# Attention times V in two layouts of its output tiles: rows interleaved by parity, or columns 0 to 127 of all 16 rows

## The chip, the core and the metric

The kernel runs on one core of one Trainium2 chip. The metric is device time in microseconds (us) of one execution; the median of several runs counts. The engines are TensorE (PE in the profile; its weight loads stand apart as PEld), VectorE (DVE), ScalarE (ACT), GpSimd (POOL) and SyncE (SP). SP and ACT also issue the transfers between the chip's main memory and the on-chip memory; all transfers run on the same 16 DMA engines.

## What is computed

The input `x` has 128 rows, 192 columns and 192 channels. After a group normalisation over all of `x`, a row attention gives each (row, column, head) a weight `sw`, and a column attention over the 192 columns, whose logits are summed over all rows, mixes the columns. The part that the change touches is the last line before the residual:

```
Q = (x @ Wq).reshape(B, R, C, H, D) * scaling * sw
K = (x @ Wk).reshape(B, R, C, H, D)
V = (x @ Wv).reshape(B, R, C, H, D)
QK = jnp.einsum('brihd,brjhd->bhij', Q, K)
attn = jax.nn.softmax(QK, axis=-1)                    # 12 heads of 192 x 192
out = jnp.einsum('bhij,brjhd->brihd', attn, V)        # 128 rows x 192 columns x 192 channels
x = x + out
```

## The kernel before, in words

**Halves.** The 12 heads of 16 channels are done in two halves `h` of 6 heads (`EH` = 96 channels). The first part of the kernel reads x, makes the statistics, and projects (L1195 and L1203) Q and K of half 0 and V of both halves, with V written to main memory. Then for each half: the logits (L1325 to L1329), softmax and transposed attention matrices `AT`, then attention times V (`attended`, L1290 and L1294). Between the two halves stands the second projection `project1` (again L1195 and L1203), which reads the transposed x back from main memory (`load_xt`, L414) in 24 chunks of 768 KB, four buffers `XT`, four chunks to a turn.

**Attention times V.** The output of a half is cut into 8 chunks `n` of `RI` = 16 rows. A chunk is 16 x 192 = 3072 (row, column) pairs of 96 channels; it lies in the tile `XO[n]` of 128 partitions x 3 thirds x 8 x 96. Before the change the flat pairs are cut into pieces of 128: third 0 has columns 0 to 127 of the even rows, third 2 columns 64 to 191 of the odd rows (held in place 1 of the tile's second index by the order `(0, 2, 1)`), and the middle third has columns 128 to 191 of an even row on partitions 0 to 63 and columns 0 to 63 of the next row on partitions 64 to 127. Each third moves between main memory and `XO[n]` in one transfer of 1024 runs of 384 bytes (384 KB).

A block is one chunk and one pair of heads; there are 24 blocks in a half (`BLOCK`; chunks 0 and 1 are interleaved, the others follow each other in threes). For each block PE makes two groups in two banks of its accumulation memory. The outer group (L1290, `t == 0`) has 2 heads x 2 thirds x 5 terms = 20 matmuls with a 128 x 128 stationary block of `AT` and 128 moving columns of V (8 rows x 16 channels). The middle group (L1294) has 2 heads x 5 terms x 2 partition halves = 20 matmuls with a 128 x 64 stationary block; the two of a pair work on different columns of the array. The five terms are high and low parts of fp16 pairs. DVE then adds each group to `XO[n]`: two instructions for the outer thirds (L1055), one for the middle (L1059).

**Order and queues.** All order is by hand, with semaphores. `load_x` (SP, L398) brings the residual x of a chunk into `XO[n]`: in half 0 chunks 0 and 1 among the last stores of V, 6 and 7 after them, then chunks 2 to 5 in turn with the loads of V (`load_v`, L428 and L430); in half 1 chunks 6 and 7 between the `load_xt` of the second projection, then 0 and 1, then 2 to 5 again with V. `store_out` (L357) writes a chunk when DVE has added its last block: the outer thirds wait for DVE's outer add, the middle third for its middle add. ACT's queue stores chunks 0 to 4, SP's queue 5 to 7. At the end of half 0 SP has first the four `load_xt` of turn 0 (which wait for the stores of chunks 0 and 1), then the stores of chunks 5 to 7, and behind these the `load_xt` of turn 1; a queue issues in program order.

Of the kernel before, what the change touches and what calls it, by code (L numbers as in the profile page):

```python
# [11 lines left out]
R, C, E, H = 128, 192, 192, 12  # L12
D = E // H
G, GC = 32, E // 32
P = 128
E1 = E - P
HALF = H // 2
EH = HALF * D
# [10 lines left out]
RI = 16  # L29
# [9 lines left out]
def row_column_attention(nc, x, wq, wk, wv, wqs, wks, res_mask, seq_mask, out):  # L39

    xs = x.rearrange("b r c e -> (b r) c e")
    xf = x.rearrange("b r c e -> (b r c) e")
    of = out.rearrange("b r c e -> (b r c) e")

    def by_thirds(flat, n, h):
        thirds = flat[n * RI * C:(n + 1) * RI * C, h * EH:(h + 1) * EH].rearrange("(q t p) e -> p t q e", t=3, p=P)
        return [thirds[:, t, :, :] for t in (0, 2, 1)]

    xt_dram = nc.dram_tensor("xt_scratch", [NCH, P, 3 * NQ * 2 * R], fp16, kind="Internal").ap()
    v0_dram = nc.dram_tensor("v0_scratch", [2, P, R, 2 * EH], fp16, kind="Internal").ap()  # L50
# [3 lines left out]
    with ctx:  # L54
# [25 lines left out]
        V0 = [q.rearrange("p w (r s e) -> p w r s e", s=2, e=EH) for q in V0]  # L80
# [67 lines left out]
        sp = [0]  # L148
# [190 lines left out]
        def attended_bank(m):  # L339

            return (m + 6) % 8
# [5 lines left out]
        opens = [min(j for j in range(NB) if BLOCK[j][0] == n) for n in range(NRC)]  # L347
        closes = [max(j for j in range(NB) if BLOCK[j][0] == n) for n in range(NRC)]

        I_FIRST, I_LAST = slice(0, P), slice(E1, C)  # L350

        def store_out(eng, h, n):
            eng.wait_ge(s_ad[h], 2 * closes[n] + 1)
            for t, third in enumerate(by_thirds(of, n, h)):
                if t == 2:
                    eng.wait_ge(s_ad[h], 2 * closes[n] + 2)
                eng.dma_start(third, XO[n][:, t, :, :]).then_inc(s_out[n], 16)  # L357

        block = ctx.enter_context(nc.Block())

# [1 line left out]
        def _(sp):  # L362
# [31 lines left out]
                                         VS[c % 2][:, :, h, k, :]).then_inc(s_vs[c % 2], 16)  # L394

            def load_x(h, n):
                for t, third in enumerate(by_thirds(xf, n, h)):
                    sp.dma_start(XO[n][:, t, :, :], third).then_inc(s_xl[n], 16)  # L398

            for c in range(3):  # L400
                store_xt(c)
# [31 lines left out]
            for h in range(2):  # L433
                if h:
                    for first, last, n in ((1, 2, 6), (2, 4, 7), (4, TURNS, 0)):
                        with sp.Fori(first, last) as t:
                            for b in range(4):
                                sp.wait_ge(s_pj[1], (4 * t + b - 3) * 2)
                                load_xt(4 * t + b, b)
                        if n:  # L440
                            sp.wait_ge(s_out[n], 48)
                            load_x(1, n)
                    sp.wait_ge(s_pj[1], NG1)
                    load_x(1, 0)
                    load_x(1, 1)
                for n in range(HALF):
                    sp.wait_ge(s_qk[h], n + 1)
                    load_v(h, n)
                    if n < len(IN_BIG):
                        load_x(h, n + 2)  # L450
                for n in range(HALF, NRC):
                    load_v(h, n)
                if h == 0:
                    for b in range(4):
                        sp.wait_ge(s_sp[b], 16 * (NCH // 4))
                    for n in range(2):
                        sp.wait_ge(s_out[n], 48)
                    for b in range(4):
                        load_xt(b, b)
                for n in range(HALF - 1, NRC):  # L460
                    store_out(sp, h, n)
            for k in range(NRC):
                sp.wait_ge(s_out[k], 96)

        @block.gpsimd
        def _(pool):
# [70 lines left out]
        def _(act):  # L537
# [167 lines left out]
            for h in range(2):  # L705
# [15 lines left out]
                if h:  # L721
                    body(0)
                    with act.Fori(1, TURNS // 2) as t:
                        body(t)
                    for n in IN_BIG:
                        act.wait_ge(s_out[n], 48)
                    with act.Fori(TURNS // 2, TURNS) as t:
                        body(t)
                    q_high1(NG1 - 1, 7)
# [23 lines left out]
        def _(dve):  # L753
# [230 lines left out]
            for h in range(2):  # L984
# [61 lines left out]

                for j, (n, hp) in enumerate(BLOCK):
                    if opens[n] == j:
                        dve.wait_ge(s_xl[n], 48 * (h + 1))
# [12 lines left out]

        @block.tensor
        def _(pe):
# [204 lines left out]
            def attended(h, m):  # L1269
                (n, hp), t = BLOCK[m // 2], m % 2  # L1270
                if t == 0:
                    pe.wait_ge(s_atl[h], 2 * hp + 2)
                    if opens[n] == m // 2:
                        pe.wait_ge(s_vl[n], 48 * (h + 1))
                when(pe, s_ad[h], m - 7)
                po = PS[:, attended_bank(m), :].rearrange("p (t q a d) -> p t q a d", t=2, a=2, d=D)

                def terms(k, odd, columns):
                    high, low = AT[:, k, :, columns], AT[:, k, :, C:2 * C][:, :, columns]
                    v0h, v0l = (V0[n][:, :, odd:RI // 2:2, s, k * D:(k + 1) * D] for s in range(2))  # L1280
                    v1 = V1[n][:, odd:RI:2, k * D:(k + 1) * D]
                    return ((high[:, 0, :], v0h), (high[:, 0, :], v0l), (low[:, 0, :], v0h),
                            (high[:, 1, :], v1), (low[:, 1, :], v1))

                for a in range(2):
                    k = 2 * hp + a
                    if t == 0:
                        for odd in range(2):
                            for i, (stationary, moving) in enumerate(terms(k, odd, I_LAST if odd else I_FIRST)):
                                ins = mm(po[:, odd, :, a, :], stationary, moving, start=i == 0, stop=i == 4)  # L1290
                    else:
                        for i, pair in enumerate(zip(terms(k, 0, slice(P, C)), terms(k, 1, slice(0, E1)))):
                            for odd, (stationary, moving) in enumerate(pair):
                                ins = mm(po[odd * E1:(odd + 1) * E1, 0, :, a, :], stationary, moving,  # L1294
                                         start=i == 0, stop=i == 4)
                ins.then_inc(s_av[h], 1)

# [71 lines left out]
```

## Time and profile before

| | us |
|---|---|
| three runs | 542.17, 542.51, 544.75; median 542.51 |
| the profiled execution, whole | 541.36 |
| its span (first to last instruction) | 539.6 |

The main stretches of the profiled execution, by the line numbers that run in them:

| stretch (us from the start of the span) | what PE does |
|---|---|
| 0 to 79 | transposes of x, statistics |
| 79 to 264 | first projection, scores |
| 267 to 312 | logits of half 0 |
| 312.6 to 360.4 | attention times V, half 0 |
| 360.3 to 437 | second projection, 6 turns of 4 chunks |
| 440.5 to 486 | logits of half 1 |
| 486.4 to 533.2 | attention times V, half 1 |
| 533.2 to 539.6 | last adds and stores |

In the views of the trace, a row of the timeline has a start, a length, the engine and line, the operation with its shape and count, and in brackets the idle time of the engine before it with what ended it. Equal neighbours are merged into one row. Rows of the chain of waits show, in order of time, what the end of the program waited for. In the tables by stretch, the last three columns are the granted clock of TensorE as a share of 2.4 GHz, the mean busy share of the 16 DMA engines (over 1 where their packets overlap), and the GB/s that they moved.

### The profile page before, as it was taken

The numbers are of one execution on the slowest core, as the hardware profiler recorded it, in microseconds if no ns is written. First come the engines' busy times: TensorE is split into PE (matmuls) and PEld (weight loads), VectorE is DVE, ScalarE is ACT, GpSimd is POOL, SyncE is SP. The second block draws the span as 40 slices with busy tenths as digits, with TensorE's granted clock in tenths as the row PEclk, the third lists the DMA queues.
The fourth block names the chain that finished last, engine by engine and source line by source line (L and its number), as shares of the span: only waits on it lengthen the run. The fifth ranks groups of instructions, "written<-read, shape, count | busy, mean of one in ns | idle before, by whom it ended". The sixth has DMA issues, their size and how long they took to land.

```text
span 539.6 us, 15989 instructions
## 1 busy us (share of the span) xinstructions
PE 502.7 (93%) x6319; PEld 393.6 (73%) x6319; DVE 390.7 (72%) x1046; ACT 276.7 (51%) x577; POOL 185.2 (34%) x232
## 2 busy tenths in 40 slices
PE   7797698899999999999899999999999979999995
PEld 6686554555555555555599988888899979998884
DVE  2689968898888888889736678655667644667763
ACT  4576776798999999995311210004565631211000
POOL 3000345585778787774300000004556540000000
PEclk9899989999999999999999999999999989999998
DMA  8999012744776667898999999999989657997997
GB/s 325 379 419 384 3 58 118 235 133 168 230 229 216 218 220 235 222 226 165 234 209 320 335 336 320 342 289 314 319 282 331 214 151 223 309 284 264 259 251 197
DMA packets 186271, 134.44 MB, mean 249 GB/s; under 512 B 168992, under 2 KB 170848, under 8 KB 186208
## 3 DMA queue, kind: packets, MB, share of 16 engines
q1 hardware_dynamic: 153664, 120.88, 71.8%
q10 hardware_dynamic: 32544, 12.68, 9.5%
q8 instruction: 44, 0.72, 0.6%
q14 instruction: 19, 0.16, 0.1%
HBM read 76.92 MB, written 56.62 MB: 247 GB/s over the span
## 4 chain that ended last, share of the span: by engine, by line
PE 76%; DVE 10%; DMA 5%; ACT 3%; issue 2%; SPq 1%; POOL 1%; DVEq 0%; POOLq 0%; ACTq 0%
PE PS L1195 23%; PE PS L1203 12%; PE PS L1290 11%; PE PS L1294 6%; DVE EXTRA L766 5%; DMA EXTRA<-in_x 4%; PE PS L1325 3%; PE PS L1328 3%; PE PS L1329 3%; PE PS L1326 3%; PE PS L1327 3%; DMA EXTRA<-xt_scratch 1%; PE PS L1156 1%; SPq L357 1%; PE PS L1079 1%
## 5 line engine op out<-in xcount | busy, mean ns | idle before, releaser
L1195 PE MATMUL PS<-WP,EXTRA 128*128 128x384 f16 (+1 forms) x1152 | 158.0, 286 | 2.6 <-DMA EXTRA<-xt_scratch 1.2
L1195 PEld LDWEIGHTS PS<-WP,EXTRA 128*128 128x128 f16 x1152 | 97.0, 98 | 46.1 <-issue 17.4
L492 POOL TENSOR_TENSOR EXTRA<-BIG,EXTRA 128x512 f16<-128x512 f32 x69 | 82.5, 1197 | 31.8 <-ACT EXTRA L597 23.9
L532 POOL TENSOR_TENSOR BIG<-EXTRA,BIG 128x384 f32 x48 | 43.8, 914 | 130.0 <-ACT BIG L708 126.6
L1203 PE MATMUL PS<-WP,EXTRA 64*128 64x384 f16 (+1 forms) x1152 | 83.1, 284 | 0.1
L1203 PEld LDWEIGHTS PS<-WP,EXTRA 64*128 64x128 f16 x1152 | 47.4, 94 | 29.4 <-issue 17.4
L498 POOL TENSOR_TENSOR BIG<-EXTRA,BIG 128x192 f16<-128x192 f32 x96 | 54.7, 570 | 36.6 <-ACT BIG L651 36.5
L1290 PE MATMUL PS<-BIG,EXTRA 128*128 128x128 f16 x960 | 61.9, 220 | 0.3
L715 ACT CAST BIG<-PS 128x384 f32 (+1 forms) x48 | 23.0, 479 | 73.3 <-PE PS L1203 64.3
L1290 PEld LDWEIGHTS PS<-BIG,EXTRA 128*128 128x128 f16 x960 | 53.8, 98 | 4.6 <-issue 0.5
L766 DVE BATCH_NORM_STATS2 EXTRA<-BIG 128x6 f32<-128x512 f32 x72 | 43.8, 678 | 16.1 <-ACT BIG L546 16.0
L1325 PE MATMUL PS<-BIG 128*128 128x192 f16 x192 | 48.8, 254 | 5.4 <-POOL BIG L532 3.2
L644 ACT CAST EXTRA<-PS 128x384 f16<-128x384 f32 x96 | 45.4, 473 | 13.9 <-PE PS L1203 6.1
L919 DVE TENSOR_TENSOR EXTRA<-PS,EXTRA 128x384 f16<-128x384 f32 x96 | 52.4, 546 | 0.0
L586 ACT ACTIVATE BIG<-BIG,small 128x512 f32<-128x512 f32 x63 | 50.9, 811 | 0.0
L993 DVE TENSOR_TENSOR EXTRA<-PS,SW 128x192 f32<-128x192 f32 x96 | 29.7, 349 | 28.2 <-ACT BIG L715 25.7
L1329 PE MATMUL PS<-BIG 128*128 128x192 f16 x192 | 48.3, 251 | 0.0
L1328 PE MATMUL PS<-BIG 128*128 128x192 f16 x192 | 48.2, 251 | 0.0
L1326 PE MATMUL PS<-BIG 128*128 128x192 f16 x192 | 48.2, 251 | 0.0
L1327 PE MATMUL PS<-BIG 128*128 128x192 f16 x192 | 48.2, 251 | 0.0
L902 DVE CAST BIG<-PS 128x192 f16<-128x192 f32 x96 | 34.0, 354 | 19.3 <-ACT EXTRA L644 18.9
L1096 PE MATMUL PS<-ident,EXTRA 128*128 128x128 f32 x288 | 37.8, 287 | 7.6 <-DMA EXTRA<-in_x 4.3
(178 smaller groups left out, 931.1 us busy)
## 6 DMA issues: line engine op xcount, KB each, us to landing
EXTRA<-in_x SPq DMA_DIRECT2D x24, 768.0 KB, 9.7
xt_scratch<-EXTRA SPq DMA_DIRECT2D x24, 768.0 KB, 3.3
BIG<-v_scratch SPq DMA_DIRECT2D x48, 384.0 KB, 5.3
EXTRA<-xt_scratch SPq DMA_DIRECT2D x24, 768.0 KB, 6.5
v_scratch<-EXTRA SPq DMA_DIRECT2D x32, 384.0 KB, 3.8
EXTRA<-in_x SPq DMA_DIRECT2D x24, 384.0 KB, 4.9
BIG<-in_x SPq DMA_DIRECT2D x24, 384.0 KB, 6.8
out_x<-BIG ACTq DMA_DIRECT2D x18, 384.0 KB, 5.6
```

Of the source, the lines that this page charges most:

```text
L492: pool.tensor_tensor(tt[:, t, 1, :].rearrange("p (q n) -> p q n", n=P), raw(c, t), tt[:, t, 0, :].rearrange("p (q n) -> p q n", n=P), ALU. ...
L498: pool.tensor_tensor(QA[:, :, C + 2 * s:C + 2 * s + 2, :], tq0(s).rearrange("p i k d -> p k i d"), QA[:, :, 2 * s:2 * s + 2, :], ALU.subtr ...
L766: ins = v.bn_stats(ST[:, t, c, :], raw(c, t))
L919: v.tensor_tensor(vs[:, :, :, 1, :], ps[:, :, 2 * EH:2 * EH + E].rearrange("p i (h e) -> p i h e", h=2), vs[:, :, :, 0, :], ALU.subtract)
L1195: ins = mm(outs[a], xt[:, t, s, q * P:(q + 1) * P], WP[:, t, w, wc], start=first and j == 0, stop=last and j == 2, skip_group_check=True)
L1203: ins = mm(outs[a], xt[rows, 1, s, q * P:(q + 1) * P], WP[rows, 1, w, wc], start=first and j == 0, stop=last and j == 2, skip_group_check= ...
L1290: ins = mm(po[:, odd, :, a, :], stationary, moving, start=i == 0, stop=i == 4)
L1325: mm(p0, q0, kh, start=first, stop=False, skip_group_check=True)
L1326: mm(p0, q0, kl, start=False, stop=last, skip_group_check=True)
L1327: mm(p1, q1, kh, start=first, stop=False, skip_group_check=True)
L1328: mm(p1, q1, kl, start=False, stop=last, skip_group_check=True)
L1329: ins = mm(p2, q2, kh, start=False, stop=last, skip_group_check=True)
```

## The change

`by_columns` takes the place of `by_thirds`. A chunk's 16 rows are two windows `w` of 8 rows. Places 0 and 1 of the tile now hold columns 0 to 127 of window 0 and window 1; the middle place holds columns 128 to 191, window 0 on partitions 0 to 63 and window 1 on partitions 64 to 127. A chunk moves in four transfers instead of three: two of 128 partitions (384 KB each) and two of 64 partitions (192 KB each). The counts that semaphore waits compare with go from 48 to 64 and from 96 to 128. All 16 rows have the same 128 output columns in the outer places, so the outer group has one stationary block for both, and its matmuls get 256 moving columns instead of 128: 10 matmuls instead of 20.

```diff
-    def by_thirds(flat, n, h):
-        thirds = flat[n * RI * C:(n + 1) * RI * C, h * EH:(h + 1) * EH].rearrange("(q t p) e -> p t q e", t=3, p=P)
-        return [thirds[:, t, :, :] for t in (0, 2, 1)]
+    def by_columns(full, tile, n, h):
+        rows = full[0, n * RI:(n + 1) * RI, :, h * EH:(h + 1) * EH].rearrange("(w r) p e -> w p r e", w=2)
+        return ([(rows[w, 0:P, :, :], tile[:, w, :, :]) for w in range(2)]
+                + [(rows[w, P:C, :, :], tile[w * E1:(w + 1) * E1, 2, :, :]) for w in range(2)])
...
-            for t, third in enumerate(by_thirds(of, n, h)):
+            for t, (there, here) in enumerate(by_columns(out, XO[n], n, h)):
                 if t == 2:
                     eng.wait_ge(s_ad[h], 2 * closes[n] + 2)
-                eng.dma_start(third, XO[n][:, t, :, :]).then_inc(s_out[n], 16)
+                eng.dma_start(there, here).then_inc(s_out[n], 16)
...
-                for t, third in enumerate(by_thirds(xf, n, h)):
-                    sp.dma_start(XO[n][:, t, :, :], third).then_inc(s_xl[n], 16)
+                for there, here in by_columns(x, XO[n], n, h):
+                    sp.dma_start(here, there).then_inc(s_xl[n], 16)
...
                     if t == 0:
-                        for odd in range(2):
-                            for i, (stationary, moving) in enumerate(terms(k, odd, I_LAST if odd else I_FIRST)):
-                                ins = mm(po[:, odd, :, a, :], stationary, moving, start=i == 0, stop=i == 4)
+                        for i, (stationary, moving) in enumerate(terms(k, slice(0, 2), slice(0, P))):
+                            ins = mm(po[:, :, a, :], stationary, moving, start=i == 0, stop=i == 4)
                     else:
-                        for i, pair in enumerate(zip(terms(k, 0, slice(P, C)), terms(k, 1, slice(0, E1)))):
-                            for odd, (stationary, moving) in enumerate(pair):
-                                ins = mm(po[odd * E1:(odd + 1) * E1, 0, :, a, :], stationary, moving,
+                        for i, pair in enumerate(zip(*(terms(k, w, slice(P, C)) for w in range(2)))):
+                            for w, (stationary, moving) in enumerate(pair):
+                                ins = mm(po[w * E1:(w + 1) * E1, 0:RI // 2, a, :], stationary, moving,
                                          start=i == 0, stop=i == 4)
```

On PE, attention times V of half 0 opens so before the change (PS is the accumulation memory, BIG holds V, EXTRA holds `AT`; L1309 to L1312 are transposes of the last attention matrix):

```order
L1290 MATMUL PS<-BIG,EXTRA 128x8x16 x20
L1294 MATMUL PS<-BIG,EXTRA 64x8x16 x20
L1290 MATMUL PS<-BIG,EXTRA 128x8x16 x20
L1294 MATMUL PS<-BIG,EXTRA 64x8x16 x20
L1290 MATMUL PS<-BIG,EXTRA 128x8x16 x20
L1294 MATMUL PS<-BIG,EXTRA 64x8x16 x20
L1309 MATMUL PS<-ident,EXTRA 128x128
```

and so with it, where the file's line numbers are 4 lower:

```order
L1286 MATMUL PS<-BIG,EXTRA 128x16x16 x10
L1290 MATMUL PS<-BIG,EXTRA 64x8x16 x20
L1286 MATMUL PS<-BIG,EXTRA 128x16x16 x10
L1290 MATMUL PS<-BIG,EXTRA 64x8x16 x20
L1286 MATMUL PS<-BIG,EXTRA 128x16x16 x10
L1290 MATMUL PS<-BIG,EXTRA 64x8x16 x20
L1305 MATMUL PS<-ident,EXTRA 128x128
```

Each outer group has half the matmuls, each twice as wide; the middle groups and their order are as before.

On SP, the stretch of half 0 that has the loads of x (EXTRA and BIG hold `XO`) and of V runs so before the change:

```order
L398 DMA EXTRA<-in_x 128x8x96 [waits xnT_stored3,projected0,v_stored1,v_stored0]
L398 DMA EXTRA<-in_x 128x8x96 x5
L428 DMA BIG<-v_scratch 128x1536 [waits logits_psum0]
L428 DMA BIG<-v_scratch 128x1536
L430 DMA BIG<-v_scratch 128x1536
L398 DMA BIG<-in_x 128x8x96 x3
```

and so with it:

```order
L395 DMA EXTRA<-in_x 128x8x96 [waits xnT_stored3,projected0,v_stored1,v_stored0]
L395 DMA EXTRA<-in_x 128x8x96
L395 DMA EXTRA<-in_x 64x8x96 x2
L395 DMA EXTRA<-in_x 128x8x96 x2
L395 DMA EXTRA<-in_x 64x8x96 x2
L425 DMA BIG<-v_scratch 128x1536 [waits logits_psum0]
L425 DMA BIG<-v_scratch 128x1536
L427 DMA BIG<-v_scratch 128x1536
L395 DMA BIG<-in_x 128x8x96 x2
L395 DMA BIG<-in_x 64x8x96 x2
```

Where three transfers of 128 partitions stood for a chunk, two of 128 and two of 64 stand; nothing moves past anything else. The stores on ACT's and SP's queues change in the same way.

## Rows read from the trace of the kernel before

**Rows 1.** The page: the span, and the chain that ended last by line.
```profile
span 539.6 us, 15989 instructions
...
PE PS L1195 23%; PE PS L1203 12%; PE PS L1290 11%; PE PS L1294 6%; DVE EXTRA L766 5%; DMA EXTRA<-in_x 4%; PE PS L1325 3%; PE PS L1328 3%; PE PS L1329 3%; PE PS L1326 3%; PE PS L1327 3%; DMA EXTRA<-xt_scratch 1%; PE PS L1156 1%; SPq L357 1%; PE PS L1079 1%
```
**Rows 2.** Chain in order of time, 355 to 392: start, us, what.
```profile
361.18 2.63 SPq L357
...
365.75 1.38 SPq L357
...
367.24 6.50 DMA EXTRA<-xt_scratch
```
**Rows 3.** Timeline of PE, 370 to 392: the two waits.
```profile
374.06 2.15 PE L1195 MATMUL PS<-WP,EXTRA 128*128 128x192 f16 x24 [1.24 <-DMA EXTRA<-xt_scratch]
...
387.89 2.15 PE L1195 MATMUL PS<-WP,EXTRA 128*128 128x192 f16 x24 [1.10 <-DVE BIG L999]
```
**Rows 4.** Timeline of SP's queue, 276 to 340: issues of x and of V.
```profile
276.92 5.69 SPq L398 DMA_DIRECT2D EXTRA<-in_x  x6
...
290.56 1.55 SPq L428 DMA_DIRECT2D BIG<-v_scratch  x2
```
**Rows 5.** Busy time by stretch, half 0; last columns clock, DMA share, GB/s.
```profile
284.00:312.00 28.00, 28.00 (x318) 26.67 (x316) 18.52 (x41) 6.04 (x15) 0.00 (x0) 1.00 1.06 329
312.00:326.00 14.00, 13.88 (x264) 12.02 (x265) 11.13 (x27) 2.04 (x5) 0.00 (x0) 1.00 1.00 347
326.00:340.00 14.00, 14.00 (x301) 12.53 (x300) 10.37 (x26) 0.00 (x0) 0.00 (x0) 1.00 1.14 298
...
361.00:369.00 8.00, 8.00 (x125) 7.53 (x124) 4.15 (x12) 3.25 (x7) 2.74 (x3) 1.00 1.24 286
```
**Rows 6.** Timeline, attention times V of half 1: PE and DVE.
```profile
527.41 1.29 PE L1290 MATMUL PS<-BIG,EXTRA 128*128 128x128 f16 x20
...
528.81 0.87 DVE L1055 SCALAR_TENSOR_TENSOR EXTRA<-PS,small,EXTRA 128x256 f32<-128x256 f32 x2 [0.70 <-PE PS L1290]
...
529.32 1.29 PE L1290 MATMUL PS<-BIG,EXTRA 128*128 128x128 f16 x20
```
**Rows 7.** Lines L1290 and L1195: ns min/median/max; one run of L1195, timeline.
```profile
L1290 PE MATMUL PS<-BIG,EXTRA x960: 216/219/231, 312.6 to 532.3; 128*128 128x128 f16 x192
...
L1195 PE MATMUL PS<-WP,EXTRA x576: 246/246/257, 360.3 to 437.0; 128*128 128x192 f16 x192
...
378.49 4.13 PE L1195 MATMUL PS<-WP,EXTRA 128*128 128x192 f16 x48
```
**Rows 8.** Busy time by stretch, end of half 1.
```profile
527.00:528.00 1.00, 1.00 (x29) 0.91 (x24) 1.00 (x3) 0.00 (x0) 0.00 (x0) 1.00 0.16 33
...
534.00:538.50 4.50, 0.00 (x0) 0.00 (x0) 0.00 (x0) 0.00 (x0) 0.00 (x0) 0.81 0.99 264
```
**Rows 9.** Busy time by stretch: stores of two queues; x loads alone.
```profile
353.00:355.00 2.00, 2.00 (x47) 1.80 (x48) 1.27 (x3) 0.00 (x0) 0.00 (x0) 1.00 1.26 288
...
279.00:285.00 6.00, 6.00 (x69) 5.60 (x68) 3.91 (x10) 1.32 (x3) 0.00 (x0) 1.00 1.17 325
```
**Rows 10.** Loads of weights: two stretches; ACT queue's bytes to 16.73; an issue.
```profile
16.25:16.73 0.48, 0.04 (x1) 0.00 (x0) 0.48 (x2) 0.40 (x1) 0.00 (x0) 1.00 1.11 340
16.73:17.50 0.77, 0.61 (x6) 0.61 (x7) 0.64 (x2) 0.77 (x1) 0.00 (x0) 1.00 1.14 281
...
q10 hardware_dynamic: 1034, 0.69, 12.9%
...
SW<-in_L_conv_Wv ACTq DMA_DIRECT2D x2, 48.0 KB, 8.3
```
**Rows 11.** Two idle times of PE (timeline), and the clock around the second.
```profile
266.68 0.30 PE L1325 MATMUL PS<-BIG 128*128 128x192 f16 x1 [2.24 <-POOL BIG L498]
...
440.48 0.30 PE L1325 MATMUL PS<-BIG 128*128 128x192 f16 x1 [3.19 <-POOL BIG L532]
...
440.00:446.00 6.00, 5.52 (x47) 5.53 (x48) 0.54 (x2) 0.00 (x0) 0.42 (x1) 0.72 1.17 324
```

More of the change, by code:

```diff
@@ L41, in row_column_attention @@
     xs = x.rearrange("b r c e -> (b r) c e")
-    xf = x.rearrange("b r c e -> (b r c) e")
-    of = out.rearrange("b r c e -> (b r c) e")
-    def by_thirds(flat, n, h):
-        thirds = flat[n * RI * C:(n + 1) * RI * C, h * EH:(h + 1) * EH].rearrange("(q t p) e -> p t q e", t=3, p=P)
-        return [thirds[:, t, :, :] for t in (0, 2, 1)]
+    def by_columns(full, tile, n, h):
+        rows = full[0, n * RI:(n + 1) * RI, :, h * EH:(h + 1) * EH].rearrange("(w r) p e -> w p r e", w=2)
+        return ([(rows[w, 0:P, :, :], tile[:, w, :, :]) for w in range(2)]
+                + [(rows[w, P:C, :, :], tile[w * E1:(w + 1) * E1, 2, :, :]) for w in range(2)])
     xt_dram = nc.dram_tensor("xt_scratch", [NCH, P, 3 * NQ * 2 * R], fp16, kind="Internal").ap()
@@ L348, in row_column_attention @@
         closes = [max(j for j in range(NB) if BLOCK[j][0] == n) for n in range(NRC)]
-        I_FIRST, I_LAST = slice(0, P), slice(E1, C)
         def store_out(eng, h, n):
             eng.wait_ge(s_ad[h], 2 * closes[n] + 1)
-            for t, third in enumerate(by_thirds(of, n, h)):
+            for t, (there, here) in enumerate(by_columns(out, XO[n], n, h)):
                 if t == 2:
                     eng.wait_ge(s_ad[h], 2 * closes[n] + 2)
-                eng.dma_start(third, XO[n][:, t, :, :]).then_inc(s_out[n], 16)
+                eng.dma_start(there, here).then_inc(s_out[n], 16)
         block = ctx.enter_context(nc.Block())
@@ L440, in _ @@
                         if n:
-                            sp.wait_ge(s_out[n], 48)
+                            sp.wait_ge(s_out[n], 64)
                             load_x(1, n)
@@ L456, in _ @@
                     for n in range(2):
-                        sp.wait_ge(s_out[n], 48)
+                        sp.wait_ge(s_out[n], 64)
                     for b in range(4):
@@ L462, in _ @@
             for k in range(NRC):
-                sp.wait_ge(s_out[k], 96)
+                sp.wait_ge(s_out[k], 128)
         @block.gpsimd
@@ L725, in _ @@
                     for n in IN_BIG:
-                        act.wait_ge(s_out[n], 48)
+                        act.wait_ge(s_out[n], 64)
                     with act.Fori(TURNS // 2, TURNS) as t:
@@ L1048, in _ @@
                     if opens[n] == j:
-                        dve.wait_ge(s_xl[n], 48 * (h + 1))
+                        dve.wait_ge(s_xl[n], 64 * (h + 1))
                     o = XO[n][:, :, :, hp * 2 * D:(hp + 1) * 2 * D]
@@ L1275, in attended, with terms @@
                 when(pe, s_ad[h], m - 7)
-                po = PS[:, attended_bank(m), :].rearrange("p (t q a d) -> p t q a d", t=2, a=2, d=D)
-                def terms(k, odd, columns):
+                po = PS[:, attended_bank(m), :].rearrange("p (q a d) -> p q a d", a=2, d=D)
+                def terms(k, ws, columns):
                     high, low = AT[:, k, :, columns], AT[:, k, :, C:2 * C][:, :, columns]
-                    v0h, v0l = (V0[n][:, :, odd:RI // 2:2, s, k * D:(k + 1) * D] for s in range(2))
-                    v1 = V1[n][:, odd:RI:2, k * D:(k + 1) * D]
+                    v0h, v0l = (V0[n][:, ws, :, s, k * D:(k + 1) * D] for s in range(2))
+                    v1 = V1[n].rearrange("p (w r) e -> p w r e", w=2)[:, ws, :, k * D:(k + 1) * D]
                     return ((high[:, 0, :], v0h), (high[:, 0, :], v0l), (low[:, 0, :], v0h),
```

## The prediction, on record before the result

> **What bounds the kernel now.** I read the page first, then the chain of waits in order of time, and then, for the places that the change touches, the timeline and the busy time by stretch. By the page PE carries the chain: the projections (L1195) and attention times V (L1290, L1294) are its longest pieces, and transfers hold only a few per cent [rows 1]. The few per cent are what matters here. In attention times V PE runs without a gap in both halves: an outer group begins every 1.91 us (529.32 less 527.41), and DVE idles 0.70 us before each pair of its outer adds [rows 6], so DVE has room and PE sets the pace.
>
> What follows each half differs. Half 1 ends with the program, and its DMA engines have room: busy share 0.16 in the microsecond at 527, before the stores of chunk 6, and only the stores of the last chunk run after PE has ended [rows 8]. Time saved on PE in half 1 is time saved. Half 0 ends in the second projection, whose turn 1 waits for its first `load_xt`: PE idles 1.24 us before 374.06, released by that transfer [rows 3]. The load was issued at 367.24, directly behind the last stores on SP's queue (issued at 361.18 to 365.75) [rows 2], whose issues last 1.4 to 2.6 us each: about what a transfer takes, so the queue takes a new one only as an old one drains. The DMA engines are at a share of 1.00 or more from 284 to 369 [rows 5], and SP's queue in this time goes from one issue to the next: the six x loads at 276.92 take 5.69 us to issue, and V's two loads at 290.56 take 1.55 [rows 4]. So from about 277 to 374 the time at which turn 1 starts is set by the sum of the DMA work, not by PE. Half 0's time saved on PE goes into that wait, and every microsecond added to the DMA work there comes out on the critical path.
>
> **The change part by part.**
>
> *Outer matmuls, fewer and wider.* A run of 20 takes 1.29 us with 0.219 us for its last: spacing (1.29 - 0.219)/19 = 56.4 ns for 128 columns. A run of 48 with 192 columns: (4.13 - 0.246)/47 = 82.6 ns [rows 7]. That is 26.2 ns for 64 columns, so 256 columns take 56.4 + 52.4 = 108.8 ns (an estimate: no such matmul is in this trace at the full clock). A block goes from 20 x 56.4 = 1.128 to 10 x 108.8 = 1.088 us, 0.04 us less. Halving the number buys little, since the columns that stream through are the same. In half 1: 24 x 0.04 = **-1.0 us**. In half 0 the same 1.0 us only lengthens the wait for turn 1: **0**.
>
> *Middle matmuls, DVE adds, waits.* Same counts and shapes; **0**. The fourth transfer of a chunk adds an issue on SP or ACT; behind the queue's backlog this is hidden, and the bytes and the number of 384-byte runs don't change.
>
> *The middle transfers, cut in halves of 64 partitions.* This is the disputed price. A whole x transfer of 393,216 bytes takes 1.21 us at the 325 GB/s of x loads alone, and a whole store 1.37 us at 288 GB/s [rows 9]. A half transfer costs between half of that (0.60 and 0.68 us: no loss) and all of it (a loss of 0.60 and 0.68 us, if half the partitions move at half the rate). The nearest row is in the loads of the weights, which have both kinds. ACT's queue loads Wq, Wk and Wv in pieces of 96, 48, 48 and 96 KB, the 48 KB ones on 64 partitions; 0.69 MB are through at 16.73, which is the first nine pieces, so that from there to about 17.5 it moves Wv's two 64-partition pieces beside SP's other loads. The rate falls from 340 to 281 GB/s [rows 10]. If half of the bytes there are 64-partition traffic, that traffic runs at 1/(2/281 - 1/340) = 239 GB/s, 1.42 times as long. The row does not isolate the cause (768-byte runs, SP's own pieces beside them), but nothing there speaks for a gain. I take 0.42: a loss of 0.25 us for each half of an x load, 0.29 us for each half of a store that has the engines to itself.
>
> The Trainium skill, SBUF — State Buffer, section "Door 1: The DMA port swizzle", speaks against the change: partitions 0 to 63 reach only half of the ports, 196 GB/s against 328 for 128 partitions at 1 MiB, and a transfer on each half one after the other gains nothing. By that ratio, 1.67, the sum below would end near 550.5 us.
>
> *Where that lands.* In half 0 all eight chunks' x is loaded ahead of turn 1's first load, by SP's queue alone: 16 halves x 0.25 = +4.0 us. Of the 16 halves of stores most run while the other queue moves whole transfers; with two queues at work the stores go at 288 GB/s, the whole engines' pace, so I count a quarter, those of chunk 2 and of chunk 7: 4 x 0.29 = +1.2. Turn 1 starts **+5.2 us** later. PE, idle 1.24 us before, idles some 7.4 (5.2 more, and 1.0 that half 0 saved). After idle times of 2.24 and 3.19 us the granted clock fell to half (1.2 GHz): the mean of the six microseconds from 440 is 0.72, so 0.28 x 6 = **+1.7 us** are lost [rows 11]; after 1.24 us it did not fall. The wait of 1.10 us at 387.89, before turn 2 [rows 3], should go, as loads have caught up by then while PE is later: **-1.1** (bounds 0 and -1.1). In half 1 x is loaded with room to spare, and the stores have room until the last chunk, whose two halves of the middle lie at the end: **+0.6**.
>
> **Sum** against the profiled execution's own 541.36 us: +5.2 + 1.7 - 1.1 + 0.6 - 1.0 = +5.4, so 546.8. That execution lies 1.15 us under the median of the three runs, 542.51; +5.4 on the median gives 547.9. **I forecast 548.0.**
>
> **The rivals.**
>
> *The halves cost no more than their bytes.* For it: the same runs, the same 16 engines, no fewer bytes in flight; the two halves follow each other on one queue and may overlap at the seam. Against it: the fall from 340 to 281. Then half 0 gains nothing up to turn 1, since the DMA work is the same; half 1 gains 1.0; the wait before turn 2 may shrink, or the wait before turn 1, then near 2.2 us, may cost clock: 541.0 to 543, likeliest 541.5, no change that can be measured. A loss under 0.15 us a half belongs here too, up to 545.
>
> *A half takes as long as a whole.* The upper bound of the same price: 16 x 0.60 + 4 x 0.68 = 12.3 for turn 1, then 12.3 + 1.7 - 1.1 + 1.4 - 1.0 = +13.3: 556.
>
> *Faster.* The other sign needs PE: if a 256-column matmul with one weight load cost only the slope, 2 x 52.4 = 104.8 ns, and the switch to the middle group (1.91 us less 1.128 and the middle's own 10 x 56.4 = 0.56, so 0.22 a block for two switches) halved as well, half 1 would gain 24 x (0.08 + 0.11) = 4.6 us: 538. It decides in half 1 alone, where PE sets the pace: an outer group under 0.98 us. Against it: the spacing already is that of streaming columns.
>
> **How the numbers follow.** About 0.5%, 2.7 us, is what a measurement of this kernel can tell from no change. Halves slower by 0.15 to 0.45 us each: 0.50, between 545 and 553, likeliest 548. No loss or a small one: 0.38, between 541 and 545. Halves as long as wholes: 0.08, 553 to 556. Faster: 0.04. The range leaves out most of the last two: 541.0 to 553.0. Faster by over 0.5%: 0.04; within 0.5%: 0.38; slower: 0.58.
>
> **What would show it.** Right: outer groups of 10 matmuls in a timeline row of about 1.25 us (9 x 108.8 ns and some 0.27 for the last); a GB/s under 300 where SP loads x alone (279 to 285 had 325); PE's wait before turn 1 at 5 to 9 us, put down to `xt_scratch`, with a clock of 0.5 for a few microseconds behind it; an unchanged pace of blocks in half 1 within 0.05 us. Wrong: x loads at 325 GB/s as before and a wait before turn 1 near 2.2 us, which means that the halves cost nothing; or a wait before turn 1 that moved while the rate stayed, which would put the loss in the issues of SP's queue instead; or a gain in half 1 of over 2 us, which would put my spacing wrong.

## The result, and the profile after

The changed kernel takes 547.38 us (median of 7 runs, 544.34 to 550.73); the kernel before, run beside it, 543.49 (7 runs, 538.31 to 548.07). The ratio is **1.0074**, with a 95% interval of 1.0037 to 1.0110: slower, by about 4 us, against a forecast of 548.0. The profiled execution of the changed kernel took 547.22 us with a span of 545.3; that of before, 541.36 with 539.6 [rows 1].

In the changed kernel all line numbers are three or four lower: stores are L354, loads of x L395, loads of XT L411, projections L1192 and L1200, the outer matmuls L1286, the middle ones L1290. The page of after, the chain by line:

```profile
span 545.3 us, 15061 instructions
...
PE PS L1192 22%; PE PS L1200 11%; PE PS L1286 10%; PE PS L1290 6%; DVE EXTRA L763 5%; DMA EXTRA<-in_x 4%; PE PS L1321 3%; PE PS L1325 3%; PE PS L1324 3%; PE PS L1323 3%; PE PS L1322 3%; DMA EXTRA<-xt_scratch 2%; ACTq L354 1%; PE PS L1153 1%; SPq L395 1%
```

Against [rows 1], `xt_scratch` has gone from 1% to 2%, and ACT's stores have come onto the chain. Where that is, the timeline of PE in the second projection of after shows (start, us, what, and in brackets the idle time before it with its releaser):

```profile
368.01 2.14 PE L1192 MATMUL PS<-WP,EXTRA 128*128 128x192 f16 x24 [2.45 <-DVE BIG L996]
...
378.87 4.02 PE L1192 MATMUL PS<-WP,EXTRA 128*128 128x192 f16 x24 [4.55 <-DMA EXTRA<-xt_scratch]
382.82 2.34 PE L1200 MATMUL PS<-WP,EXTRA 64*128 64x192 f16 x48
385.09 4.13 PE L1192 MATMUL PS<-WP,EXTRA 128*128 128x192 f16 x48
```
```profile
418.87 2.15 PE L1192 MATMUL PS<-WP,EXTRA 128*128 128x192 f16 x24 [0.86 <-DMA EXTRA<-xt_scratch]
```

The wait before turn 1, 1.24 us in [rows 3], is now 4.55, and the 24 matmuls behind it take 4.02 us where 24 take 2.15 elsewhere: they run at half the clock. The wait of 1.10 before turn 2 is gone, and a new one of 0.86 stands at 418.87. The wait at 368.01, in turn 0, was not foreseen; it is taken up below.

Why `xt_scratch` comes late is seen where SP loads x alone. Busy time by stretch of after; the last three columns are PE's clock, the DMA share and GB/s. The first row lies in the two outer transfers of chunk 6, the second in the two halves of its middle tile:

```profile
281.20:283.20 2.00, 2.00 (x20) 1.60 (x19) 0.69 (x3) 0.79 (x2) 0.00 (x0) 1.00 1.17 324
283.40:284.90 1.50, 1.50 (x22) 1.50 (x20) 1.43 (x4) 0.00 (x0) 0.00 (x0) 1.00 1.27 238
```

The same shows in 40 slices, 281 to 287 in after, and 279 to 285 in before, where all transfers have 128 partitions:

```profile
DMA  9999999999999999999999999999999999999999
GB/s 328 315 323 323 328 328 328 325 328 320 323 325 328 315 323 297 213 243 271 233 215 210 218 248 251 276 317 323 320 315 325 323 328 422 307 305 307 305 307 305
```
```profile
GB/s 325 328 328 325 320 320 323 328 328 328 325 328 313 328 328 328 328 328 317 328 323 323 323 328 325 328 323 328 323 325 317 328 328 328 325 328 318 323 323 328
```

The engines are busy throughout (every DMA digit is 9), and yet the rate falls to 210 to 276 GB/s as long as the halves run: each packet takes longer (the 384-byte packets of x take 22 ns throughout in before; in 279 to 286 of after the slowest twentieth take 39 or more, and from 283.5 to 284.75 the median is 31 to 39). Two halves, 393,216 bytes, at 238 GB/s take 1.65 us, against 1.21 for a whole transfer: **0.22 us lost for each half**.

The way of the 5.7 us, each mark measured from the first logits of half 0 (266.68 before, 267.21 after, both named by their wait of 2.2 us, [rows 11]):

| | before | after | difference |
|---|---|---|---|
| turn 1 of the second projection starts | 107.38 | 111.66 | +4.28 |
| from there to the next row of 48 at the same line (378.49, 385.09) | 4.43 | 6.22 | +1.79 |
| wait before turn 2 | 1.10 | 0 | -1.10 |
| wait before 418.87 | 0 | 0.86 | +0.86 |
| first logits of half 1 (440.48, 446.85) | 173.80 | 179.64 | +5.84 |
| attention times V of half 1, first to last matmul | 46.83 | 46.25 | -0.58 |
| from there to the end | 6.45 | 6.31 | -0.14 |

The fifth row is the sum of the four above it. With the last two rows and the 0.53 us by which the first logits themselves were later, this makes 5.65 us. Those 0.53 us are there ahead of any changed transfer: the stores of V at L393 and L390 begin a row at 225.33 in before and 225.86 in after.

### The profile page after: what moved, and what is told of

It is laid out like the page before. It is cut to its first block, busy times and chain, and to the rows that moved or that the text cites. A ratio compares the mean times of both kernels' runs of the same rounds, so it can differ in the third digit from the quotient of the medians.

```text
span 545.3 us, 15061 instructions
## 1 busy us (share of the span) xinstructions
PE 505.2 (93%) x5839; PEld 386.5 (71%) x5839; DVE 391.8 (72%) x1046; ACT 276.3 (51%) x577; POOL 185.1 (34%) x232
## 4 chain that ended last, share of the span: by engine, by line
PE 74%; DVE 11%; DMA 6%; ACT 2%; issue 2%; SPq 1%; ACTq 1%; POOL 1%; DVEq 0%; POOLq 0%
PE PS L1192 22%; PE PS L1200 11%; PE PS L1286 10%; PE PS L1290 6%; DVE EXTRA L763 5%; DMA EXTRA<-in_x 4%; PE PS L1321 3%; PE PS L1325 3%; PE PS L1324 3%; PE PS L1323 3%; PE PS L1322 3%; DMA EXTRA<-xt_scratch 2%; ACTq L354 1%; PE PS L1153 1%; SPq L395 1%
## 5 line engine op out<-in xcount | busy, mean ns | idle before, releaser
L1192 PE MATMUL PS<-WP,EXTRA 128*128 128x384 f16 (+1 forms) x1152 | 160.0, 289 | 8.1 <-DMA EXTRA<-xt_scratch 5.4
L1192 PEld LDWEIGHTS PS<-WP,EXTRA 128*128 128x128 f16 x1152 | 98.5, 99 | 52.0 <-issue 26.0
L1200 PE MATMUL PS<-WP,EXTRA 64*128 64x384 f16 (+1 forms) x1152 | 83.1, 284 | 0.0
L1200 PEld LDWEIGHTS PS<-WP,EXTRA 64*128 64x128 f16 x1152 | 47.6, 94 | 29.3 <-issue 17.3
L1286 PE MATMUL PS<-BIG,EXTRA 128*128 128x256 f16 x480 | 60.7, 274 | 0.3
L1286 PEld LDWEIGHTS PS<-BIG,EXTRA 128*128 128x128 f16 x480 | 43.0, 98 | 9.0 <-issue 0.5
L1093 PE MATMUL PS<-ident,EXTRA 128*128 128x128 f32 x288 | 39.6, 296 | 5.9 <-DMA EXTRA<-in_x 3.8
```

The costliest lines, as they stand in the source:

```text
L1192: ins = mm(outs[a], xt[:, t, s, q * P:(q + 1) * P], WP[:, t, w, wc], start=first and j == 0, stop=last and j == 2, skip_group_check=True)
L1200: ins = mm(outs[a], xt[rows, 1, s, q * P:(q + 1) * P], WP[rows, 1, w, wc], start=first and j == 0, stop=last and j == 2, skip_group_check= ...
L1286: ins = mm(po[:, :, a, :], stationary, moving, start=i == 0, stop=i == 4)
```

## The experiments

Two theories on the loss: **H**, a transfer on 64 partitions on one side of SBUF moves slower; **N**, each further transfer costs, on whatever partitions. Times below are ratios to the kernel before, run beside each, with 95% intervals. One profiled execution varies by about 2 us up to turn 1 even with the loads of x whole: V's last load in half 0 ("V" below) lands 63.4, 63.5, 64.4, 65.0 and 65.1 us behind the first logits in the five such profiles (before, and runs e2, e4, e11, e5). The profile of before is at the low end of that, so only differences beyond it count.

**The middle cut in halves, or in rows, with the old matmuls.**

```
-        return [thirds[:, t, :, :] for t in (0, 2, 1)]
+        outer = [(thirds[:, t, :, :], tile[:, i, :, :]) for i, t in enumerate((0, 2))]
+        return outer + [(thirds[ps, 1, qs, :], tile[ps, 2, qs, :]) for ps, qs in cut]
+
+    HALVES_ = [(slice(0, E1), slice(0, RI // 2)), (slice(E1, P), slice(0, RI // 2))]
+    ROWS_ = [(slice(0, P), slice(0, RI // 4)), (slice(0, P), slice(RI // 4, RI // 2))]
...
```

In e1 `cut` is `HALVES_` for x and for out, in e2 `ROWS_` for both, in e3 `HALVES_` for x alone, in e4 `HALVES_` for out alone.

> The kernel before with one edit: its middle transfer, for x and for out, is cut in two of 64 partitions each (four transfers a chunk, matmuls as before). Theory H (a transfer on 64 partitions moves slower): nearly the whole loss of the change is here without its matmuls; V's last load lands some 4.5 us later than before (16 halves at 0.28), turn 1 of the second projection starts 4 to 5 us later, part of the packets of x take more than the 22 ns of before, and the ratio to before is 1.008 to 1.012, as half 1 gains nothing. Rival N (each further transfer costs, on whatever partitions): the same here, so that it takes the next run to tell them apart. Rival M (the loss comes with the wide matmuls or their order): 1.000.

> The kernel before, its middle transfer for x and for out cut in two of 128 partitions and half the rows each: as many transfers as in the changed kernel, none on 64 partitions. Theory H: no loss, ratio 0.998 to 1.002, packets of x at 22 ns throughout, turn 1 starts within 0.7 us of before. Rival N (number of transfers): as with the halves, 1.008 to 1.012, V's last load 4 to 5 us later.

e1: **1.0076** (1.0040 to 1.0112). e2: **1.0026** (0.9993 to 1.0059). V's last load: 69.3 us with halves, 63.5 with rows. Turn 1 starts 112.9 and 108.3 us behind the first logits, against 107.4 before. The rate of the x loads, 281 to 287 in e1 and 283 to 289 in e2:

```profile
GB/s 238 328 325 328 323 325 318 328 328 328 320 328 323 328 320 325 323 325 318 292 228 238 279 236 215 220 230 236 264 297 325 328 323 419 305 307 305 307 302 307
```
```profile
GB/s 205 307 328 328 328 325 323 310 325 328 328 328 328 323 328 323 325 325 323 313 323 328 328 323 320 328 328 328 328 325 323 409 302 307 307 307 307 307 315 315
```

With the halves the fall to 215 to 279 is there without the wide matmuls; with as many transfers of 128 partitions there is none. H holds, and the loss of the change is in its transfers. e2's interval excludes the 1.008 of N but leaves room for a small price of a further transfer.

> The kernel before with only the loads of x cut in halves of 64 partitions in the middle; the stores stay whole. By the prediction's terms x carries 4.0 of the 5.2 us before turn 1: V's last load 4 to 4.5 us later, turn 1 some 4 us later, ratio 1.007 to 1.009. Rival S (the stores carry it): 1.002 or less.

> The kernel before with only the stores of out cut in halves of 64 partitions in the middle; the loads of x stay whole. By the prediction's terms: turn 1 starts 1.2 us later, the end of half 1 costs 0.6 more, ratio 1.002 to 1.004. If a store on 64 partitions loses nothing, as the GB/s of the stretch with stores from two queues in the changed kernel suggest (286, against 285 before): 1.000, turn 1 within 0.3 us of before.

e3: **1.0074** (1.0032 to 1.0116). e4: **1.0018** (0.9981 to 1.0055). The loads carry what can be measured. In e4's profile turn 1 does start 1.3 us later than before, where 0.3 at most was expected of stores that lose nothing; 1.0 of it is there already at V's last load, so it lies in the scatter named above. For the stores this is one stretch each, of before and of after, with the last stores of half 0, from two queues and in after of both kinds:

```profile
361.00:367.00 6.00, 6.00 (x98) 5.69 (x96) 2.85 (x9) 2.66 (x6) 1.03 (x2) 1.00 1.25 285
```
```profile
366.00:372.00 6.00, 3.99 (x72) 3.87 (x72) 4.55 (x15) 3.63 (x10) 2.70 (x4) 1.00 1.25 286
```

With two queues at work the stores move at 285 GB/s, halves among them or not. At the end of half 1, where SP's queue stores alone, the halves do dip. The rows are of before, and of after in its whole and in its half transfers:

```profile
536.50:537.50 1.00, 0.00 (x0) 0.00 (x0) 0.00 (x0) 0.00 (x0) 0.00 (x0) 0.66 1.18 322
```
```profile
541.30:542.80 1.50, 0.00 (x0) 0.00 (x0) 0.00 (x0) 0.00 (x0) 0.00 (x0) 1.00 1.16 319
542.80:543.80 1.00, 0.00 (x0) 0.00 (x0) 0.00 (x0) 0.00 (x0) 0.00 (x0) 0.93 0.93 224
```

For about a microsecond the rate is 224 GB/s in place of some 320, and here the share falls too. It costs next to nothing: from its first issue to its last landing the last chunk takes 5.58 us, against 5.71 before and 5.52 in e5, which has the same matmuls and whole transfers.

**Number of partitions, or their side.** The middle's 64 partitions taken between each other:

```
-    HALVES_ = [(slice(0, E1), slice(0, RI // 2)), (slice(E1, P), slice(0, RI // 2))]
+    HALVES_ = [(slice(0, P, 2), slice(0, RI // 2)), (slice(1, P, 2), slice(0, RI // 2))]
```

That is e9, made from e3. In e12 all three transfers of a chunk's x are cut so (the edit is against e3, whose cut of the middle is taken out):

```
-                    sp.dma_start(here, there).then_inc(s_xl[n], 16)
+                    for side in range(2):
+                        sp.dma_start(here[side:P:2], there[side:P:2]).then_inc(s_xl[n], 16)
```

> The kernel before, the middle third's load of x cut in two of 64 partitions that lie between each other: the even ones and the odd ones, in place of 0 to 63 and 64 to 127; the stores stay whole. If a half loses because it has 64 rows of SBUF and not 128 (half as many partitions in flight), V's last load comes 5 to 6 us later, as with the lower and upper halves (69.3 us behind the first logits, 63.4 before), ratio 1.006 to 1.009. If it loses because its 64 partitions lie on one side of SBUF, the loss is gone: 63.4 to 64.5, ratio 0.999 to 1.002.

> The kernel before, every one of a chunk's three loads of x cut in even and odd partitions: six transfers of 64 interleaved partitions, 48 such halves ahead of turn 1 where the run with the middle alone had 16; the stores stay whole. It is to settle that run, whose time showed no loss and whose profile a late V. If a transfer loses because it has 64 partitions (0.28 us each), V's last load comes some 13 us later than before (76 us behind the first logits) and the ratio is 1.015 to 1.025. If it loses only where the 64 lie on one side, the packets stay at 22 ns, V's last load stays within 63.4 to 66 and the ratio is 0.998 to 1.003. If each transfer more has a price of its own of 0.1 us (24 more in half 0), 2.4 us later, ratio 1.003 to 1.006.

e9: **1.0005** (0.9958 to 1.0052). Its x loads, 280 to 286, the halves among them:

```profile
GB/s 225 328 328 328 328 320 318 325 325 328 323 328 328 325 313 325 328 323 318 325 323 323 310 328 328 328 328 328 328 325 295 328 325 328 320 328 328 325 318 424
```

No fall: 64 partitions that lie on both sides load at the full 324 GB/s, and 19 of 20 packets take 22 ns at most. The slow packet comes from the side, not from the number. The rate shows this; by the times alone e9 and e3 (1.0074) are not apart, since their intervals overlap. Its profiled execution (548.39 us, among the longest of its 12) shows V late all the same, at 67.7, but in another way: in 300 to 304 the DMA share is 0.63, while SP's four issues of x take 7.35 us.

```profile
294.11 7.35 SPq L403 DMA_DIRECT2D BIG<-in_x  x4
...
300.00:304.00 4.00, 4.00 (x52) 4.00 (x51) 3.15 (x7) 0.89 (x2) 0.00 (x0) 1.00 0.63 169
```

e12: **1.0079** (1.0043 to 1.0116), V at 66.9. It fits none of its three expectations: too little for 0.28 us a half, too much for none, and above the 1.003 to 1.006 of a price of 0.1 us. Its x loads, 284 to 290:

```profile
DMA  7999988977899999999999779999999989999999
GB/s 187 277 282 254 223 202 233 266 210 197 225 264 325 282 274 318 312 310 282 284 266 225 187 197 225 284 305 274 277 320 312 277 231 277 261 363 251 274 277 264
```

Here the share falls along with the rate (digits of 7 and 8, mean 1.02 over 284.3 to 289.3), where it stayed at 1.27 in the changed kernel: engines without work, not slow packets (19 of 20 take 22 ns at most). So N has a part too when all transfers are small: 24 more in half 0, V 1.7 to 3.5 us later, 0.07 to 0.15 us each. How much of it there is with 8 more remains open: e9's time says none, its profile some. A third of e12's loss would be 1.0026, which is what e2 has, and e2's interval reaches from none to over twice that.

**The wide matmuls alone.** The kernel of after, its transfers those of before:

```
-        rows = full[0, n * RI:(n + 1) * RI, :, h * EH:(h + 1) * EH].rearrange("(w r) p e -> w p r e", w=2)
...
+        return [(thirds[:, t, :, :], tile[:, i, :, :]) for i, t in enumerate((0, 2, 1))]
```

> The changed matmuls (10 of 256 columns for an outer group) with the transfers of before, three of 128 partitions a chunk: x and out then stand at other places than the tiles expect, so that the values are permuted, at the same work. By the prediction's terms: outer groups about 0.03 to 0.04 us shorter each, 0.7 to 1.0 us less in half 1, up to as much in half 0 that goes into the wait before turn 1 of the second projection; turn 1 starts within 0.7 us of before and the ratio is 0.996 to 1.000. The rival of a faster PE: an outer group under 0.98 us, ratio 0.990 to 0.994.

e5 (the changed matmuls, the three transfers of before): **0.9980** (0.9943 to 1.0018). Attention times V of half 1 takes 46.25 us, as in the changed kernel, against 46.83. The gain is there and is 0.58 us, too small for the run's time to show; the rival of a faster PE falls. Turn 1 starts 2.3 us later than before, where 0.7 at most was expected; 1.8 of it is there at V's last load, again in the scatter.

**Other orders of the halves.**

In e6:

```
-                for there, here in by_columns(x, XO[n], n, h):
+                outer0, outer1, lower, upper = by_columns(x, XO[n], n, h)
+                for there, here in (outer0, lower, outer1, upper):
```

In e7 SP leaves out the fourth transfer of chunks 2 to 5, and ACT issues it behind its own wait for the same logits:

```
                     act.wait_ge(s_qk[h], k + 1)
+                    if k < len(IN_BIG):
+                        there, here = by_columns(x, XO[k + 2], k + 2, h)[3]
+                        act.dma_start(here, there).then_inc(s_xl[k + 2], 16)
...
```

> The changed kernel, x loaded in the order outer, lower half, outer, upper half, instead of the two halves one behind the other. If a half loses because the next one, which could fill what it leaves idle, also stands behind a whole transfer in the queue, nothing changes: ratio 1.006 to 1.010, V's last load within 0.7 us of the changed kernel's 68.3 us behind the first logits. If two neighbouring halves already overlap in the changed kernel, the order is worse: 1 to 4 us later, 1.010 to 1.015. If a whole transfer on each side covers a half, V's last load comes 2 to 5 us sooner and the ratio is 1.000 to 1.004.

> The changed kernel, the upper half of x of chunks 2 to 5 is issued by ACT on its own queue at the time when SP may issue the lower half, so that two queues hold a half each. If halves lose because one queue has only one half of the partitions in flight, the four chunks of half 0 win back up to 0.28 x 8 = 2.2 us: V's last load 66 us behind the first logits (68.3 changed, 63.4 before), ratio 1.002 to 1.005. If the loss is in each half by itself, 68.3 stays and the ratio is 1.006 to 1.010. ACT's issues stand ahead of its own casts; where they block, the logits of half 0 take longer, and the ratio is over 1.010.

e6: **1.0118** (1.0071 to 1.0166), V at 71.7 against 68.3: worse, so the two halves one behind the other do overlap in part. Its x loads fall to 156, deeper than the 210 of the changed kernel (284 to 290; the loads of x begin in the fifth slice):

```profile
GB/s 0 79 90 46 156 230 282 323 328 328 323 328 310 328 325 287 261 261 164 156 164 223 302 312 320 323 323 325 318 289 271 207 225 233 236 202 225 266 310 323
```

The Trainium skill, SBUF — State Buffer, section "Door 1: The DMA port swizzle", gives 196 GB/s for 64 partitions on one side and 328 for 128. The whole transfers here agree (324), the pair of halves lies between (238), and a half among wholes goes below 196 for moments (164 and 156 in e6). By its map the even partitions reach every port, and e9's 324 agrees.

e7: **1.0023** (0.9986 to 1.0060). The time lies where a gain was expected, but its profile shows none (V at 70.1, not 66) and a new wait: ACT, with its own issues, ends its stores later, and PE waits 4.3 us for ACT's casts in turn 0. Whether two queues help is not settled by this.

**What lies behind the wait before turn 1.**

```
+                        if first == 1:
+                            store_out(sp, 0, NRC - 1)
...
-                for n in range(HALF - 1, NRC):
+                for n in range(HALF - 1, NRC - 1 + h):
```

In e8 chunk 7's stores so stand behind turn 1's four loads on SP's queue.

> The changed kernel, SP issues the four loads of turn 1 of the second projection ahead of the stores of chunk 7 and not behind them. If the end of the DMA work in half 0 is what delays turn 1, four stores of 1.37 us go out of its way: turn 1 starts 4 to 5 us sooner (at 107 us behind the first logits, 111.7 in the changed kernel, 107.4 before), its wait falls under 1 us, the half clock of 6.8 us is gone, and the time is 5 to 7 us under the changed kernel's: ratio to before 0.994 to 0.999. If it was the queue's own issues, the same; if turn 1's buffers come free only when the stores are out anyway, nothing: 1.006 to 1.010.

e8: **1.0093** (1.0063 to 1.0123), where 0.994 to 0.999 was expected. Turn 1 starts without a wait, at about 107 us as expected; PE's timeline:

```profile
367.89 2.14 PE L1194 MATMUL PS<-WP,EXTRA 128*128 128x192 f16 x24 [2.46 <-DVE BIG L998]
...
378.20 4.13 PE L1194 MATMUL PS<-WP,EXTRA 128*128 128x192 f16 x48
...
391.77 2.58 PE L1194 MATMUL PS<-WP,EXTRA 128*128 128x192 f16 x15 [5.26 <-DMA EXTRA<-xt_scratch]
```

The wait moved to turn 2, whose loads stand behind chunk 7's stores and the load of x for chunk 6 (SP's queue: 374.80 for 5.88 us, 380.72 for 3.96, then turn 2's at 385.08). The first logits of half 1 start 179.8 us behind those of half 0, 179.6 in the changed kernel. So the debt is one sum of DMA work, and a new order ahead of turn 1 only changes where it is paid. This also tells of the wait in turn 0. In the changed kernel PE waits 2.45 us there, by the chain for ACT's casts, which come behind ACT's store issues:

```profile
360.86 2.72 ACTq L354
...
363.62 1.61 ACTq L354
...
365.27 0.49 ACT BIG L712
...
368.01 2.14 PE PS L1192 x24
...
372.81 5.82 DMA EXTRA<-xt_scratch
```

That time cost nothing: the load of turn 1, issued at 372.81, decided in any case. The chain of waits leads into it from PE, but SP issued it 0.13 us after the issue of its last store ended (371.77 for 0.91 us), much as in before (367.24, after 365.75 and 1.38), and the chunk whose buffer it takes had been projected some 10 us earlier.

**The work spread out.** Chunk 4's stores go from ACT to SP; the stores of chunks 6 and 7 and the loads of x for them go one by one behind the last load of turn 1 and those of turns 2 to 5 (SP's loop over the turns is written out for it):

```
+                    for c in range(4, 4 * TURNS):
+                        sp.wait_ge(s_pj[1], (c - 3) * 2)
+                        load_xt(c, c % 4)
+                        if c >= 7 and other:
+                            other.pop(0)()
...
```

> The changed kernel with the DMA work of half 0 pulled out from in front of the second projection: the stores of chunk 4 go from ACT's queue to SP's; the stores of chunks 6 and 7 and the loads of x of half 1 for them go one by one behind the loads of turns 1 to 5, and not in one piece ahead of them. If the sum of DMA work up to turn 2 is what the halves hurt, the waits before turns 1 and 2 fall under 0.5 us, ACT's late casts no longer hold turn 0 (2.4 us in the changed kernel), the half clock behind turn 1 is gone, and the second logits start 170 to 172 us behind the first (179.6 changed, 173.8 before): ratio to before 0.990 to 0.995. If the pieces between the loads delay these in turn, PE waits on xt_scratch in turns 2 to 5, some 0.8 us a turn, and the ratio is 0.996 to 1.003.

> The kernel before with the same order of stores and loads as in the run with the changed kernel. It has waits of 1.24 and 1.10 us to lose there: the second logits start 171 to 172.5 us behind the first (173.8 before), ratio 0.995 to 0.998. If the wide matmuls are worth their 0.8 to 1.0 us in each half, this one ends 1.5 to 2 us behind the changed kernel with this order; if the halves still cost something, it ends level or ahead.

e10 (on the changed kernel): **0.9877** (0.9836 to 0.9918), 539.50 us. e11 (on the kernel before): **0.9875** (0.9830 to 0.9919), 537.90 us. Both beat both kernels (the changed one, at 1.0074, did not run beside them). What PE waits for in the whole second projection (us in total, times, longest; e10, then e11, whose only wait is the one before the logits):

```profile
PE PS L1335 <- POOL BIG L543: 3.2, 1, 3.2
PE PS L1206 <- DMA EXTRA<-xt_scratch: 1.8, 2, 1.6
PE PS L1214 <- DMA EXTRA<-xt_scratch: 0.2, 1, 0.2
```
```profile
PE PS L1339 <- POOL BIG L546: 3.2, 1, 3.2
```

The logits of half 1 start 170.2 and 169.7 us behind those of half 0, 179.6 and 173.8 without the spread. The halves are still slow in e10 (212 to 266 GB/s in five slices of 0.3 us, 287.5 to 289), but nearly all of their time is hidden. Between the two there is no difference that these runs can tell. Of e10's wait of 1.62 us before turn 1 it is not shown that the halves cause it: its clock did not fall at the first logits, as it did in e11, and its second projection starts 2.1 us sooner behind them (90.4 and 92.5), of which the wide matmuls give some 0.6. The rows are of e10 and of e11:

```profile
271.80:277.80 6.00, 6.00 (x73) 6.00 (x74) 1.68 (x6) 0.00 (x0) 0.00 (x0) 1.00 1.24 257
```
```profile
267.30:273.30 6.00, 5.96 (x54) 5.97 (x55) 1.71 (x7) 0.00 (x0) 0.00 (x0) 0.73 1.13 263
```

e11 gains more than was expected. Its two waits account for 2.34 of the 4.1 us up to the second logits, and 1.2 are there already where the second projection starts; the rest of the gain, which the time of the run confirms, is not explained.

## Why the prediction was right

By its own steps:

- *A half loses 0.25 us in a load of x.* Measured 0.22 in chunk 6, at 238 GB/s where 239 was estimated from the weights [rows 10]; over all 16 halves V's last load gives 0.27 (68.6 us on average in after, e1, e8 and e10, 64.3 in the five profiles with whole loads). The ratio here is 324/238 = 1.36. That the mixed row of the weights came so near is in part luck: it mixed other runs and pieces, as the prediction says. The Trainium skill's ratio (SBUF — State Buffer, "Door 1: The DMA port swizzle"), 1.67, was too large for two halves in a row. That the two halves follow each other is part of this price (e6).
- *Stores lose 0.29 us in four halves, +1.2.* Wrong: they lose no time that shows (286 GB/s, 285 before; e4 1.0018; from V's last load to turn 1 it is 43.4 us in after and 44.0 in before). The price of loads was carried over to stores, where no row showed it. The dip to 224 GB/s with one queue, at the end of half 1, cost less than 0.1 us.
- *Turn 1 starts +5.2 later.* Measured +4.28, against 4.0 predicted for the loads alone: 16 x 0.22 = 3.5 or 16 x 0.27 = 4.3, and the difference lies within the 2 us by which profiles differ up to there.
- *The clock costs 1.7.* Measured 1.79: the granted clock is 0.57 over 376 to 384, the eight microseconds around the end of the wait of 4.55 us, against 0.72 over six in [rows 11]. It was low for longer than assumed, but part of that lay in the wait itself. Such a fall is not certain: in the profiles of e2 and e10 the clock stayed at 1.00 behind the same waits of 2.25 and 3.19 us at the logits.

```profile
376.00:384.00 8.00, 5.13 (x48) 4.64 (x50) 0.00 (x0) 0.17 (x1) 0.43 (x1) 0.57 1.02 391
```

- *PE idles some 7.4 us before turn 1.* It idles 4.55 there and 2.45 in turn 0: 7.0 in all. The place was wrong for a third of it, since ACT's queue was left out: like SP's, it takes a new store only as an old one drains (issues of 2.72 and 1.61 us, shown with e8), and ACT's casts stand behind its issues. It cost nothing only because the transfer came later still.
- *The wait before turn 2 goes, -1.1.* Right. The wait of 0.86 at 418.87, behind the loads of x for chunk 7, was missed; the sum counted the x of half 0 alone, while the loads of turns 2 and 4 each stand behind four transfers of x for half 1, two of them halves.
- *A wide matmul takes 108.8 ns, -1.0 in half 1.* The sign is right, the size was not: 0.58. A row of ten takes 1.27 us with 0.273 for its last, so (1.27 - 0.273)/9 = 110.8 ns. Two nanoseconds too few, ten times a block: a gain of 0.02 us, not 0.04. A difference of two large terms is very sensitive to their slope.

```profile
531.41 1.27 PE L1286 MATMUL PS<-BIG,EXTRA 128*128 128x256 f16 x10
...
533.29 1.27 PE L1286 MATMUL PS<-BIG,EXTRA 128*128 128x256 f16 x10
```

  A pair of groups takes 1.88 us, against 1.91 in [rows 6].
- *The end of half 1, +0.6.* Measured -0.14, nothing, as the stores lose nothing.

The sum of +5.4 on the profiled execution, and the 5.65 measured there, agree because the errors cancel: stores and end together 2.0 too much, PE's gain 0.4 too large, and 0.9 and 0.5 not foreseen. That 548.0 lies so near 547.38 is luck too: the kernel before took 543.49 beside the changed one, not the 542.51 that the forecast started from, so the medians are 3.9 us apart and not 5.4. The mechanism, a loss in the loads of halves that comes out before turn 1, stands by e1, e2 and e3 and by the rate in e9; that the number of transfers has a part of up to a third is not excluded (e2, e12).

## What to carry to other kernels

A layout that makes a matmul wider is paid for where its tiles are moved: look at which partitions each transfer touches, and at whether that stretch is bound by the DMA engines, before counting instructions saved. When an engine waits for a transfer behind a long train, moving one piece of the train moves the wait; spreading the train over a stretch with room (a DMA share of 0.77 over 388 to 436 in before) removes it, here about 1% for either layout. And a slow transfer has two looks: engines fully busy at a low rate (slow packets) or a share that falls with the rate (engines without work).

## What was not expected of the hardware

- Loads into 64 partitions on one side of SBUF fall from 324 to 238 GB/s at a DMA share of 1.27, and loads into 64 interleaved partitions stay at 324. Stores from the same partitions stay at 286 with two queues; with one they dip to 224 for a microsecond, at a share of 0.93.
- Cutting every load of x in two interleaved ones leaves the engines partly idle (share 1.02, 266 GB/s over 284.3 to 289.3, against 1.17 and 325 in [rows 9]).
- The same waits of PE, 2.25 us before the first logits and 3.19 before the second, were followed by a granted clock of 0.72 to 0.77 over the next six microseconds in 12 and 11 of the 14 profiles. In e2 and e10 it stayed at 1.00 behind both, in e12 behind the second.
